# A ring for the transposed fields, longer product rings, and TensorE's sums in groups of two to four units

## The chip, the cores and the metric

The kernel runs on one core of a Trainium2 chip. The metric is the device time of one execution in microseconds. Five engines work beside each other, each through its own list of instructions in the order written: TensorE (PE), VectorE (DVE), ScalarE (ACT), GpSimd (POOL, here the issuer of gathers) and SyncE (SP, here the issuer of the other transfers). They meet only at semaphores.

## The reference

A recommendation model: 32 embedding tables of 64 columns are looked up for 1024 samples, all pairs of the 32 fields (496) go through a bilinear form of their own, and the 496 results with 16 dense inputs feed a network of three layers.

```python
e = stack([tbl_f[ids[:, f]] for f in range(32)], axis=1)      # 1024 x 32 x 64
p, q = e[:, ROW_IDX], e[:, COL_IDX]                            # the 496 pairs i < j
z = einsum('bne,hne,bnh->bn', p, kernel, q)                    # kernel: 64 x 496 x 64
h = concatenate([z, dense_ctx], axis=1)                        # 512 inputs
h = maximum(h @ W_top1 + b_top1, 0)                            # 512
h = maximum(h @ W_top2 + b_top2, 0)                            # 256
y = h @ W_top3                                                 # 1024 x 1
```

Everything is float32.

## The kernel before

The 1024 samples are taken in four chunks of 256. POOL gathers the rows of all fields (256 indirect transfers, four fields or one "quad" after the other), and TensorE transposes each quad (`transpose_quad`, line 520), so that a couple of fields lies across the 128 partitions with the samples along the row. VectorE copies the result from PSUM to `emb` (`keep_quad`, line 426).

The pairs of a chunk are cut into 64 units of equal arithmetic, in the order of the list `UNITS`. `bilinear` issues a unit's matmuls into one of three pairs of PSUM banks (`bil`, a ring of `BIL_RING` = 3 that the transposes share), and VectorE's `multiply` takes it out again, times the second field of each pair. There are three kinds:

- `inner` (8 in a chunk): the pairs within a quad, 8 recorded matmuls (line 552) and three VectorE products (lines 454 to 458);
- `fields` (32): pairs with the samples along the row, 8 recorded matmuls (line 552) and one product into `prod` (line 447);
- `batch` (24): pairs with the samples across the partitions, 4 recorded matmuls (line 537) and one product into `rows_prod` (line 438).

What is left is a sum over 64 elements. For a batch unit ScalarE does it by 16 activations with an accumulated output (`sum_rows`, line 365), or VectorE by a reduction (line 480) for the units that `SUM_UNITS` names. For the 40 inner and fields units of a chunk TensorE does it, by matmuls with a selector of ones: `reduce_batch`, line 572, four recorded matmuls a unit, that is two of the kernel's, each on 32 columns of the array. `slot_row` says which: the units alternate between column tiles 0, 1 and column tiles 2, 3. Before, these sums come in 20 batches of two units, each batch issued `REDUCE_LAG` = 3 units after its last unit.

When a chunk's sums are done, `turn` (line 587) transposes ScalarE's and VectorE's sums on TensorE. It waits for the last ScalarE sum of the chunk, and stands in TensorE's order a few units into the next chunk. The three layers of a chunk (`head`, lines 597 to 607) go between units of the next chunk, at `PIECE_UNITS`; those of the last chunk stand at the end (lines 633 to 665).

The order of TensorE's work around the change is written out by these tables: at each unit `u` the quads that are due are transposed, the unit is issued, then a batch of sums, then a piece of the head. Each use of `bil` waits until VectorE has emptied the pair of banks used three uses before. A chunk's unit `inner` of quad 1 waits for VectorE's copy of that quad's transposes.

Of the kernel before, what the change touches and what calls it, by code (L numbers as in the profile page):

```python
# [9 lines left out]
ALU = mybir.AluOpType  # L10
# [33 lines left out]

ORDER = ["", "ff", "bbbb", "bfbbfb", "fffbbfff", "bfbbfffbff", "bbffbbffbfbf", "fffbffbbfbffff"]


def unit_list():  # L50
# [21 lines left out]

SUM_UNITS = [8, 52]
VECTOR_SUMS = {max(v for v in range(NB) if BATCHED[v] <= u) for u in SUM_UNITS}
NV, NA = len(VECTOR_SUMS), NB - len(VECTOR_SUMS)

BIL_RING, PROD_RING, ROWS_RING, IN_RING = 3, 6, 4, 4
BATCH_UNITS = 2  # L80
BATCHES = NS // BATCH_UNITS
GROUP_BATCHES = 32 // BATCH_UNITS
REDUCE_LAG = 3
SUM_LAG = 2
SEL_WIDTH = 30 + 32
K_DMA = 8


def summed_before(u):
# [104 lines left out]

def reduce_unit(b):

    return unit_at((b + 1) * BATCH_UNITS - 1) + REDUCE_LAG


REDUCED_AT = {reduce_unit(b): b for b in range(BATCHES * CHUNKS) if reduce_unit(b) < NUNIT}  # L200
# [1 line left out]


PIECES = ["l1a", "l1b", "l2", "l3"]
PIECE_UNITS = [9, 14, 32, 56]
KEPT_BEFORE = [0, 2, 4, 6]
KEPT = 7

# [11 lines left out]
def interaction_tower(nc, ids, tables, dense_rows, k_blocks, w1, b1, w2, b2, w3, ident, selector, y):  # L220
    ctx = ExitStack()
    with ctx:
# [16 lines left out]
        w3_sb = sb("w3_sb", [P, MT2])  # L239
        k_sb = sb("k_sb", [P, 2 * NPART, P])  # L240
        gathered = sb("gathered", [P, 2, CT, FIELDS * EMBED])
        emb = sb("emb", [P, 2, COUPLES, CHUNK])
        prod = sb("prod", [P, PROD_RING, 2, BANK])
        rows_prod = sb("rows_prod", [P, ROWS_RING, 16, EMBED])
        inner = sb("inner", [P, IN_RING, 2, CHUNK])
# [39 lines left out]
        def inner_batch(n):  # L285

            q, k = divmod(n, QUADS)
            return summed_before(q * NU + FIRST_OF[k]) // BATCH_UNITS

        @block.sync  # L290
        def _(sp):
# [59 lines left out]
        def _(act):  # L351
# [40 lines left out]
            for u in range(NUNIT):  # L392
                if u >= SUM_LAG and UNITS[(u - SUM_LAG) % NU][0] == "batch":
                    sum_rows(u - SUM_LAG)
                if u in REDUCED_AT:
                    q, b = divmod(REDUCED_AT[u], BATCHES)
                    if b in (GROUP_BATCHES - 1, BATCHES - 1):
                        copy_z(q, b // GROUP_BATCHES)
# [19 lines left out]
        def _(dve):  # L418
            def keep_quad(n):
                q, k = divmod(n, QUADS)  # L420
                dve.wait_ge(quad_transposed, n + 1)

                banks = bil[BANKS_OF["quad", n]][:, :, 0:CHUNK].rearrange("p s (x b) -> p x s b", b=EMBED)
                out = emb[:, q % 2, 2 * k:2 * k + 2, :].rearrange("p c b -> p (c b)")
                out = out.rearrange("p (x s b) -> p x s b", s=2, b=EMBED)
                dve.tensor_copy(out, banks).then_inc(emb_kept, 1)  # L426

            def multiply(u):
                q, (kind, part, t) = u // NU, UNITS[u % NU]
                k, m, c = PARTS[part]  # L430
                x_y, e = bil[BANKS_OF["unit", u]], emb[:, q % 2, :, :]
                dve.wait_ge(unit_done, u + 1)
                if kind == "batch":
                    v = batched_before(u)
                    if v >= ROWS_RING:
                        free_rows(v - ROWS_RING)
                    row = gathered[:, q % 2, t, 2 * c * EMBED:(2 * c + 8) * EMBED].unsqueeze(1)
                    dve.tensor_tensor(rows_prod[:, v % ROWS_RING, :, :].rearrange("p (j x) h -> p j (x h)", j=2),  # L438
                                      x_y[:, :, :], row.to_broadcast([P, 2, BANK]), ALU.mult).then_inc(unit_multiplied, 1)
                    return  # L440
                a = summed_before(u)
# [9 lines left out]
                a, b = 2 * k, 2 * k + 1  # L451
                if n >= IN_RING:
                    dve.wait_ge(batch_reduced, inner_batch(n - IN_RING) + 1)
                dve.tensor_tensor(out[:, 0, :].rearrange("p (j b) -> p j b", j=2), x_y[:, :, 0:CHUNK],  # L454
                                  e[:, a:a + 1, :].to_broadcast([P, 2, CHUNK]), ALU.mult)
                dve.tensor_tensor(inner[EMBED:P, n % IN_RING, 0, :], x_y[EMBED:P, 0, CHUNK:BANK],  # L456
                                  e[EMBED:P, b, :], ALU.mult)
                dve.tensor_tensor(inner[0:EMBED, n % IN_RING, 0, :], x_y[0:EMBED, 1, CHUNK:BANK],  # L458
                                  e[0:EMBED, a, :], ALU.mult).then_inc(unit_multiplied, 1)

            def free_rows(v):

# [40 lines left out]
        def _(pe):  # L503
# [21 lines left out]
            def bilinear(u):  # L525
# [196 lines left out]
```

## Time and profile before

| | |
|---|---|
| median of 3 runs | 434.41 us (434.13 to 434.64) |
| the profiled execution | 433.44 us |
| its span, first to last instruction | 431.6 us, so 1.8 us lie around it |
| PE busy | 386.8 us, 90% |
| ACT busy | 350.7 us, 81% |
| DVE busy | 338.0 us, 78% |
| POOL busy | 242.2 us, 56% |
| granted TensorE clock | 0.999 of full speed |

The 40 slices of the page show POOL issuing gathers for the first 30, and PE at 9 tenths in nearly all slices from the seventh on. The trace has four points that cut the run into stretches: the four `turn`s start at 130.62, 227.34, 324.06 and 419.07 us. The first chunk (up to 130.62) starts slowly, since the gathers arrive one quad after the other, and has no head pieces in it. The second and third stretch take 96.72 us each. A busy PE is not a measure of work done: matmul ends are modelled, so the rows below are read by their starts. What a thing costs on PE is the time from its start to the next thing's start.

### The profile page before, as it was taken

The numbers are of one execution on the slowest core, as the hardware profiler recorded it, in microseconds if no ns is written. First come the engines' busy times: TensorE is split into PE (matmuls) and PEld (weight loads), VectorE is DVE, ScalarE is ACT, GpSimd is POOL, SyncE is SP. The second block draws the span as 40 slices with busy tenths as digits, with TensorE's granted clock in tenths as the row PEclk, the third lists the DMA queues.
The fourth block names the chain that finished last, engine by engine and source line by source line (L and its number), as shares of the span: only waits on it lengthen the run. The fifth ranks groups of instructions, "written<-read, shape, count | busy, mean of one in ns | idle before, by whom it ended". The sixth has DMA issues, their size and how long they took to land.

```text
span 431.6 us, 9783 instructions
## 1 busy us (share of the span) xinstructions
PE 386.8 (90%) x2912; PEld 218.4 (51%) x2912; DVE 338.0 (78%) x369; ACT 350.7 (81%) x2850; POOL 242.2 (56%) x260
## 2 busy tenths in 40 slices
PE   0224789999989999999989999999989999999997
PEld 0113344546454655645554655655555655655556
DVE  1033898999988879699888879699888869799841
ACT  1000799999994999999983999999974999999971
POOL 5777777777777777777777777777770000000000
PEclk9999999999999999999999999999999999999999
DMA  4677992111111111111111111111110000000000
GB/s 120 157 168 162 200 261 58 30 25 29 28 27 29 30 26 30 25 29 30 25 30 30 25 30 29 26 30 25 30 30 2 1 2 1 2 3 0 2 2 0
DMA packets 13637, 19.29 MB, mean 45 GB/s; under 512 B 5584, under 2 KB 6928, under 8 KB 13584
## 3 DMA queue, kind: packets, MB, share of 16 engines
q0 software_dynamic: 8192, 8.40, 10.0%
q1 hardware_dynamic: 5392, 10.27, 10.0%
q8 instruction: 23, 0.38, 0.3%
q14 instruction: 30, 0.25, 0.2%
HBM read 18.65 MB, written 0.00 MB: 43 GB/s over the span
## 4 chain that ended last, share of the span: by engine, by line
PE 66%; ACT 20%; POOL 5%; DVE 3%; issue 3%; DMA 2%; DVEq 0%
PE bil L552 24%; ACT rows_prod L365 19%; PE bil L537 16%; PE z_ps L572 13%; PE side_ps L597 5%; POOL gathered L345 5%; PE side_ps L602 3%; DVE prod L447 2%; PE bil L520 2%; DMA gathered<-in_tbl,ids_sb 1%; PE bil L633 1%; PE z_ps L587 1%; PE bil L657 1%; PE side_ps L607 1%; DVE rows_prod L438 1%
## 5 line engine op out<-in xcount | busy, mean ns | idle before, releaser
L365 ACT ACTIVATE rows_prod<-rows_prod 128x64 f32<-128x64 f32 x1408 | 336.1, 245 | 56.0 <-DVE rows_prod L438 56.0
L345 POOL DMA_INDIRECT gathered<-in_tbl,ids_sb x256 | 242.0, 945 | 80.3 <-issue 77.7
L365 ACT ACTIVATION_READ_ACCUMULATOR rows_prod<-rows_prod 128x1 f32 x1408 | 269.3, 191 | 0.0
L552 PE MATMUL bil<-emb,k_sb 64*128 64x256 f32 x1280 | 163.9, 392 | 6.3 <-DVE emb L426 5.5
L447 DVE TENSOR_TENSOR prod<-bil,emb 128x1024 f32<-128x1024 f32 x128 | 151.3, 1214 | 8.6 <-PE bil L552 8.4
L552 PEld LDWEIGHTS bil<-emb,k_sb 64*128 64x128 f32 x1280 | 120.0, 190 | 65.2 <-issue 38.8
L438 DVE TENSOR_TENSOR rows_prod<-bil,gathered 128x1024 f32<-128x1024 f32 x96 | 115.2, 1215 | 28.2 <-PE bil L537 27.8
L537 PE MATMUL bil<-k_sb,emb 64*128 64x512 f32 x384 | 99.6, 610 | 1.6 <-DVE inner L458 1.6
L572 PE MATMUL z_ps<-prod,sel_sb 128*32 128x512 f32 x576 | 86.0, 604 | 0.2 <-ACT z_sb L375 0.2
L537 PEld LDWEIGHTS bil<-k_sb,emb 64*128 64x128 f32 x384 | 33.5, 186 | 32.0 <-DVE prod L447 16.9
L520 PE MATMUL bil<-ident_sb,gathered 64*128 64x64 f32 x256 | 15.2, 241 | 33.1 <-DMA gathered<-in_tbl,ids_sb 33.1
L426 DVE COPY emb<-bil 128x512 f32<-128x512 f32 x32 | 21.8, 681 | 29.3 <-PE bil L520 29.2
L520 PEld LDWEIGHTS bil<-ident_sb,gathered 64*128 64x128 f32 x256 | 11.5, 145 | 55.7 <-issue 37.1
L572 PEld LDWEIGHTS z_ps<-prod,sel_sb 128*32 128x32 f32 x576 | 12.7, 108 | 42.4 <-issue 14.7
L454 DVE TENSOR_TENSOR prod<-bil,emb 128x512 f32<-128x512 f32 x32 | 21.9, 683 | 10.3 <-PE bil L552 10.3
L572 PE MATMUL z_ps<-inner,sel_sb 128*32 128x512 f32 x64 | 25.2, 604 | 0.0
L597 PE MATMUL side_ps<-z_sb,w_sb 128*128 128x256 f32 x96 | 22.3, 386 | 0.0
L597 PEld LDWEIGHTS side_ps<-z_sb,w_sb 128*128 128x128 f32 x96 | 17.7, 190 | 4.2 <-issue 2.0
L375 ACT ACTIVATE z_sb<-z_ps 128x512 f32<-128x512 f32 x8 | 4.8, 594 | 12.9 <-PE z_ps L587 11.0
L456 DVE TENSOR_TENSOR inner<-bil,emb 64x256 f32<-64x256 f32 x32 | 13.7, 427 | 0.4
L458 DVE TENSOR_TENSOR inner<-bil,emb 64x256 f32<-64x256 f32 x32 | 13.3, 417 | 0.4
L602 PE MATMUL side_ps<-h_sb,w_sb 128*128 128x256 f32 x48 | 11.2, 386 | 0.0
(31 smaller groups left out, 72.3 us busy)
## 6 DMA issues: line engine op xcount, KB each, us to landing
k_sb<-in_k_blocks SPq DMA_DIRECT2D x24, 256.0 KB, 4.8
gathered<-in_tbl,ids_sb POOLq DMA_INDIRECT x256, 2.4
k_sb<-in_k_blocks SPq DMA_DIRECT2D x8, 192.0 KB, 5.8
inner<-in_dense_rows SPq DMA_DIRECT2D x64, 1.0 KB
w_sb<-in_w SPq DMA_DIRECT2D x1, 1024.0 KB
k_sb<-in_k_blocks SPq DMA_DIRECT2D x8, 64.0 KB, 4.7
w_sb<-in_w SPq DMA_DIRECT2D x1, 512.0 KB
ids_sb<-in_ids SPq DMA_DIRECT2D x1, 128.0 KB, 2.0
```

Source lines behind the costliest of these rows:

```text
L345: pool.indirect_dma_start(gathered[:, q % 2, t, field * EMBED:(field + 1) * EMBED], None, tables[field], bass.IndirectOffsetOnAxis(ap=ids_ ...
L365: last = act.activation(row, row, ACT.Copy, accum_out=z_rows[:, t, half, col:col + 1])
L426: dve.tensor_copy(out, banks).then_inc(emb_kept, 1)
L438: dve.tensor_tensor(rows_prod[:, v % ROWS_RING, :, :].rearrange("p (j x) h -> p j (x h)", j=2), x_y[:, :, :], row.to_broadcast([P, 2, BANK ...
L447: dve.tensor_tensor(out, x_y[:, :, :], both.to_broadcast([P, 2, BANK]), ALU.mult)\
L454: dve.tensor_tensor(out[:, 0, :].rearrange("p (j b) -> p j b", j=2), x_y[:, :, 0:CHUNK], e[:, a:a + 1, :].to_broadcast([P, 2, CHUNK]), ALU ...
L520: last = pe.transpose(bil[BANKS_OF["quad", n]][:, s, at:at + EMBED], gathered[rows, q % 2, t, (2 * k + c) * P:(2 * k + c + 1) * P], ident_ ...
L537: last = pe.matmul(out[:, s, :], e[rows, m, t * P:(t + 1) * P], k_sb[rows, 2 * part:2 * part + 4, :].rearrange("p n h -> p (n h)"), start= ...
L552: last = pe.matmul(out[:, s, i * CHUNK:(i + 1) * CHUNK], k_sb[rows, n, :], e[rows, j, :], start=True, stop=True)
L572: last = pe.matmul(z_ps[32 * col:32 * (col + 1), :], sel_sb[:, 30 - r:62 - r], moving, start=r == 0, stop=bank == 0 and r == 30, tile_posi ...
L597: last = pe.matmul(bank[:, j * CHUNK:(j + 1) * CHUNK], w1_sb[:, g, n * P:(n + 1) * P], z_sb[:, g, :], start=g == 0, stop=g == GROUPS - 1)
L602: last = pe.matmul(bank[:, n * CHUNK:(n + 1) * CHUNK], w2_sb[:, g, n * P:(n + 1) * P], h1_sb[:, g, :], start=g == 0, stop=g == MT1 - 1)
```

## The change

- `emb` becomes a ring of 20 couples (`EMB_RING`, `emb_at`) in place of two chunks of 16. The room goes to the rings of products: `PROD_RING` 6 to 8, `ROWS_RING` 4 to 5.
- TensorE's sums come in 14 groups of 4, 3, 2, 2, 4, 2, 3, 2, 3, 3, 4, 3, 3 and 2 units (`SUM_GROUPS`) in place of 20 batches of two. Each is still issued three units after its last unit.
- The units of quads 3 to 7 stand in another order (`ORDER`); there are as many of each kind.
- VectorE sums three batch units of a chunk (`SUM_UNITS`) in place of two, so ScalarE sums 21 in place of 22.
- The head's second piece moves from unit 14 to 17, the others by one unit.

```diff
-ORDER = ["", "ff", "bbbb", "bfbbfb", "fffbbfff", "bfbbfffbff", "bbffbbffbfbf", "fffbffbbfbffff"]
+ORDER = ["", "ff", "bbbb", "fbbfbb", "bffffffb", "bffbbbfbfb", "bbfbffffbfff", "ffbbfbfbffffff"]
...
-SUM_UNITS = [8, 52]
+SUM_UNITS = [17, 30, 54]
...
-BIL_RING, PROD_RING, ROWS_RING, IN_RING = 3, 6, 4, 4
-BATCH_UNITS = 2
-BATCHES = NS // BATCH_UNITS
-GROUP_BATCHES = 32 // BATCH_UNITS
+BIL_RING, PROD_RING, ROWS_RING, IN_RING = 3, 8, 5, 4
+
+SUM_GROUPS = [4, 3, 2, 2, 4, 2, 3, 2, 3, 3, 4, 3, 3, 2]
+BATCHES = len(SUM_GROUPS)
+GROUP_ENDS = [sum(SUM_GROUPS[:b + 1]) for b in range(BATCHES)]
+GROUP_BATCHES = GROUP_ENDS.index(32) + 1
...
+EMB_RING = COUPLES + 4
+
+def emb_at(q, c):
+    return (q * COUPLES + c) % EMB_RING
...
+def group_end(b):
+    q, r = divmod(b, BATCHES)
+    return q * NS + GROUP_ENDS[r]
...
-    return unit_at((b + 1) * BATCH_UNITS - 1) + REDUCE_LAG
+    return unit_at(group_end(b) - 1) + REDUCE_LAG
...
-PIECE_UNITS = [9, 14, 32, 56]
+PIECE_UNITS = [9, 17, 33, 57]
...
-        emb = sb("emb", [P, 2, COUPLES, CHUNK])
+        emb = sb("emb", [P, EMB_RING, CHUNK])
...
                 if a >= PROD_RING:
-                    dve.wait_ge(batch_reduced, (a - PROD_RING) // BATCH_UNITS + 1)
+                    dve.wait_ge(batch_reduced, group_of(a - PROD_RING) + 1)
...
             def reduce_batch(b):
-                pe.wait_ge(unit_multiplied, unit_at((b + 1) * BATCH_UNITS - 1) + 1)
+                pe.wait_ge(unit_multiplied, unit_at(group_end(b) - 1) + 1)
                 q, r = divmod(b, BATCHES)
-                if b and r % GROUP_BATCHES == 0:
+                if b and r in (0, GROUP_BATCHES):
                     pe.wait_ge(z_copied, 2 * q + r // GROUP_BATCHES)
-                for a in range(b * BATCH_UNITS, (b + 1) * BATCH_UNITS):
+                for a in range(group_end(b) - SUM_GROUPS[r], group_end(b)):
```

In the listings of order the matmuls are those the kernel writes, each recorded twice in the trace; in the changed kernel line 542 is the transposes, 559 a batch unit, 574 a fields or inner unit, 594 the sums. First, TensorE's order from unit 53 of the first chunk to its end; before:

```order
L537 MATMUL bil<-k_sb,emb 128x512 x2
L552 MATMUL bil<-emb,k_sb 128x256 x4
L572 MATMUL z_ps<-prod,sel_sb 32x512 x4
L552 MATMUL bil<-emb,k_sb 128x256 x4
L537 MATMUL bil<-k_sb,emb 128x512 x4
L572 MATMUL z_ps<-prod,sel_sb 32x512 x4
L552 MATMUL bil<-emb,k_sb 128x256 x4
L537 MATMUL bil<-k_sb,emb 128x512 x2
L552 MATMUL bil<-emb,k_sb 128x256 x8
L572 MATMUL z_ps<-prod,sel_sb 32x512 x4
```

And now, from unit 51 to the same place:

```order
L574 MATMUL bil<-emb,k_sb 128x256 x4
L559 MATMUL bil<-k_sb,emb 128x512 x4
L574 MATMUL bil<-emb,k_sb 128x256 x4
L594 MATMUL z_ps<-prod,sel_sb 32x512 x3
L594 MATMUL z_ps<-inner,sel_sb 32x512
L594 MATMUL z_ps<-prod,sel_sb 32x512 x4
L559 MATMUL bil<-k_sb,emb 128x512 x2
L574 MATMUL bil<-emb,k_sb 128x256 x4
L559 MATMUL bil<-k_sb,emb 128x512 x2
L574 MATMUL bil<-emb,k_sb 128x256 x16
L594 MATMUL z_ps<-prod,sel_sb 32x512 x6
```

The sums of two units at a time (four matmuls) have become one of four units (eight matmuls) and one of three (six matmuls), and between these two now stand seven units without a break. In the later chunks a piece of the head stands in these seven.

Second, TensorE's order across the boundary of two chunks, right behind the rows above: transposes of quad 0 of the next chunk, the last two units and the next chunk's unit 0, sums, transposes of quad 1, unit 1, transposes of quad 2, unit 2, sums, and the turn. Before:

```order
L520 MATMUL bil<-ident_sb,gathered 128x64 x8
L552 MATMUL bil<-emb,k_sb 128x256 x12
L572 MATMUL z_ps<-prod,sel_sb 32x512 x4
L520 MATMUL bil<-ident_sb,gathered 128x64 x8
L552 MATMUL bil<-emb,k_sb 128x256 x4
L520 MATMUL bil<-ident_sb,gathered 128x64 x8
L552 MATMUL bil<-emb,k_sb 128x256 x4
L572 MATMUL z_ps<-prod,sel_sb 32x512 x4
L587 MATMUL z_ps<-ident_sb,z_rows 32x128 x16
```

And now:

```order
L542 MATMUL bil<-ident_sb,gathered 128x64 x8
L574 MATMUL bil<-emb,k_sb 128x256 x12
L594 MATMUL z_ps<-prod,sel_sb 32x512 x6
L542 MATMUL bil<-ident_sb,gathered 128x64 x8
L574 MATMUL bil<-emb,k_sb 128x256 x4
L542 MATMUL bil<-ident_sb,gathered 128x64 x8
L574 MATMUL bil<-emb,k_sb 128x256 x4
L594 MATMUL z_ps<-prod,sel_sb 32x512 x4
L609 MATMUL z_ps<-ident_sb,z_rows 32x128 x16
```

Nothing has changed its place here; the sums behind the next chunk's unit 0 are of three units (six matmuls) in place of two.

## Rows read from the trace of the kernel before

**Rows 1.** The stretches; columns are named in the first line.
```profile
core 0: us, PE busy (x) PEld busy (x) DVE busy (x) ACT busy (x) POOL busy (x), PEclk, DMA share, GB/s
85.00:130.62 45.62, 43.77 (x352) 23.20 (x350) 43.24 (x48) 45.57 (x379) 34.34 (x38) 1.00 0.14 28
227.34:324.06 96.72, 95.18 (x732) 53.93 (x728) 83.73 (x92) 87.54 (x713) 72.22 (x77) 1.00 0.15 28
```
**Rows 2.** The chain around the first turn: start, us, what.
```profile
115.29 15.29 ACT rows_prod L365 x128
130.62 1.08 PE z_ps L587 x32
```
**Rows 3.** PE's timeline, pitches of units, sums and transposes: start, us, what.
```profile
298.54 2.86 PE L552 MATMUL bil<-emb,k_sb 64*128 64x256 f32 x24
301.33 0.63 PE L572 MATMUL z_ps<-prod,sel_sb 128*32 128x512 f32 x3
...
328.00 1.99 PE L537 MATMUL bil<-k_sb,emb 64*128 64x512 f32 x8
329.92 1.06 PE L572 MATMUL z_ps<-prod,sel_sb 128*32 128x512 f32 x8
330.91 0.47 PE L520 MATMUL bil<-ident_sb,gathered 64*128 64x64 f32 x8
331.21 1.94 PE L537 MATMUL bil<-k_sb,emb 64*128 64x512 f32 x8
332.99 1.03 PE L552 MATMUL bil<-emb,k_sb 64*128 64x256 f32 x8
```
**Rows 4.** The chain near the end: two batches of sums together, then the turn.
```profile
417.22 1.85 PE z_ps L572 x16
419.07 0.92 PE z_ps L587 x32
```
**Rows 5.** PE's timeline at a batch of sums cut in two by a wait.
```profile
66.42 1.04 PE L572 MATMUL z_ps<-prod,sel_sb 128*32 128x512 f32 x2
67.48 0.62 PE L572 MATMUL z_ps<-inner,sel_sb 128*32 128x512 f32 x1
67.48 0.62 PE L572 MATMUL z_ps<-prod,sel_sb 128*32 128x512 f32 x2
...
68.47 1.12 PE L537 MATMUL bil<-k_sb,emb 64*128 64x512 f32 x3
```
**Rows 6.** PE's timeline at a chunk's first units.
```profile
318.98 0.46 PE L520 MATMUL bil<-ident_sb,gathered 64*128 64x64 f32 x8
320.98 1.13 PE L552 MATMUL bil<-emb,k_sb 64*128 64x256 f32 x8 [1.54 <-DVE emb L426]
```
**Rows 7.** DVE's timeline at the same place, and at the transposes at 330.91.
```profile
318.78 0.68 DVE L454 TENSOR_TENSOR prod<-bil,emb 128x512 f32<-128x512 f32 x1
...
320.25 0.67 DVE L426 COPY emb<-bil 128x512 f32<-128x512 f32 x1
...
331.45 0.68 DVE L426 COPY emb<-bil 128x512 f32<-128x512 f32 x1
```
**Rows 8.** DVE's timeline, pace of products and a reduction.
```profile
299.81 3.47 DVE L447 TENSOR_TENSOR prod<-bil,emb 128x1024 f32<-128x1024 f32 x3
303.21 1.20 DVE L480 TENSOR_REDUCE z_rows<-rows_prod 128x16 f32<-128x1024 f32 x1
```
**Rows 9.** PE's timeline at a run of five units.
```profile
79.19 1.13 PE L537 MATMUL bil<-k_sb,emb 64*128 64x512 f32 x4
80.16 2.76 PE L552 MATMUL bil<-emb,k_sb 64*128 64x256 f32 x24
82.78 1.13 PE L537 MATMUL bil<-k_sb,emb 64*128 64x512 f32 x4
```
**Rows 10.** DVE's timeline at the same place.
```profile
81.51 3.47 DVE L447 TENSOR_TENSOR prod<-bil,emb 128x1024 f32<-128x1024 f32 x3
```
**Rows 11.** PE's timeline at the transposes of quad 4, first chunk.
```profile
58.74 0.46 PE L520 MATMUL bil<-ident_sb,gathered 64*128 64x64 f32 x8 [0.84 <-DMA gathered<-in_tbl,ids_sb]
```

More of the change, by code:

```diff
@@ L71 @@
 FIRST_PARTS = [UNITS[u][1] for u in BATCHED if UNITS[u][2] == 0]
-SUM_UNITS = [8, 52]
+SUM_UNITS = [17, 30, 54]
 VECTOR_SUMS = {max(v for v in range(NB) if BATCHED[v] <= u) for u in SUM_UNITS}
 NV, NA = len(VECTOR_SUMS), NB - len(VECTOR_SUMS)
-BIL_RING, PROD_RING, ROWS_RING, IN_RING = 3, 6, 4, 4
-BATCH_UNITS = 2
-BATCHES = NS // BATCH_UNITS
-GROUP_BATCHES = 32 // BATCH_UNITS
+BIL_RING, PROD_RING, ROWS_RING, IN_RING = 3, 8, 5, 4
+SUM_GROUPS = [4, 3, 2, 2, 4, 2, 3, 2, 3, 3, 4, 3, 3, 2]
+BATCHES = len(SUM_GROUPS)
+GROUP_ENDS = [sum(SUM_GROUPS[:b + 1]) for b in range(BATCHES)]
+assert GROUP_ENDS[-1] == NS
+GROUP_BATCHES = GROUP_ENDS.index(32) + 1
 REDUCE_LAG = 3
@@ L103, in vector_sums_before, with group_of @@
     return q * NV + sum(1 for x in VECTOR_SUMS if x < r)
+def group_of(a):
+    q, r = divmod(a, NS)
+    return q * BATCHES + sum(1 for end in GROUP_ENDS if end <= r)
+def group_end(b):
+    q, r = divmod(b, BATCHES)
+    return q * NS + GROUP_ENDS[r]
 def unit_at(a):
@@ L287, in inner_batch @@
             q, k = divmod(n, QUADS)
-            return summed_before(q * NU + FIRST_OF[k]) // BATCH_UNITS
+            return group_of(summed_before(q * NU + FIRST_OF[k]))
         @block.sync
@@ L397, in _ @@
                     if b in (GROUP_BATCHES - 1, BATCHES - 1):
-                        copy_z(q, b // GROUP_BATCHES)
+                        copy_z(q, int(b == BATCHES - 1))
                 if u == min(HEAD_AT):
@@ L423, in keep_quad @@
                 banks = bil[BANKS_OF["quad", n]][:, :, 0:CHUNK].rearrange("p s (x b) -> p x s b", b=EMBED)
-                out = emb[:, q % 2, 2 * k:2 * k + 2, :].rearrange("p c b -> p (c b)")
+                at = emb_at(q, 2 * k)
+                out = emb[:, at:at + 2, :].rearrange("p c b -> p (c b)")
                 out = out.rearrange("p (x s b) -> p x s b", s=2, b=EMBED)
@@ L430, in multiply @@
                 k, m, c = PARTS[part]
-                x_y, e = bil[BANKS_OF["unit", u]], emb[:, q % 2, :, :]
+                x_y = bil[BANKS_OF["unit", u]]
                 dve.wait_ge(unit_done, u + 1)
@@ L443, in multiply @@
                 if a >= PROD_RING:
-                    dve.wait_ge(batch_reduced, (a - PROD_RING) // BATCH_UNITS + 1)
+                    dve.wait_ge(batch_reduced, group_of(a - PROD_RING) + 1)
                 if kind == "fields":
-                    both = e[:, c:c + 2, :].rearrange("p c b -> p (c b)").unsqueeze(1)
+                    both = emb[:, emb_at(q, c):emb_at(q, c) + 2, :].rearrange("p c b -> p (c b)").unsqueeze(1)
                     dve.tensor_tensor(out, x_y[:, :, :], both.to_broadcast([P, 2, BANK]), ALU.mult)\
@@ L450, in multiply @@
                 n = q * QUADS + k
-                a, b = 2 * k, 2 * k + 1
+                a, b = emb_at(q, 2 * k), emb_at(q, 2 * k + 1)
                 if n >= IN_RING:
@@ L454, in multiply @@
                 dve.tensor_tensor(out[:, 0, :].rearrange("p (j b) -> p j b", j=2), x_y[:, :, 0:CHUNK],
-                                  e[:, a:a + 1, :].to_broadcast([P, 2, CHUNK]), ALU.mult)
+                                  emb[:, a:a + 1, :].to_broadcast([P, 2, CHUNK]), ALU.mult)
                 dve.tensor_tensor(inner[EMBED:P, n % IN_RING, 0, :], x_y[EMBED:P, 0, CHUNK:BANK],
-                                  e[EMBED:P, b, :], ALU.mult)
+                                  emb[EMBED:P, b, :], ALU.mult)
                 dve.tensor_tensor(inner[0:EMBED, n % IN_RING, 0, :], x_y[0:EMBED, 1, CHUNK:BANK],
-                                  e[0:EMBED, a, :], ALU.mult).then_inc(unit_multiplied, 1)
+                                  emb[0:EMBED, a, :], ALU.mult).then_inc(unit_multiplied, 1)
             def free_rows(v):
@@ L532, in bilinear @@
                 wait_banks(("unit", u))
-                out, e = bil[BANKS_OF["unit", u]], emb[:, q % 2, :, :]
+                out = bil[BANKS_OF["unit", u]]
                 if kind == "batch":
@@ L536, in bilinear @@
                         rows = slice(s * EMBED, (s + 1) * EMBED)
-                        last = pe.matmul(out[:, s, :], e[rows, m, t * P:(t + 1) * P],
+                        last = pe.matmul(out[:, s, :], emb[rows, emb_at(q, m), t * P:(t + 1) * P],
                                          k_sb[rows, 2 * part:2 * part + 4, :].rearrange("p n h -> p (n h)"),
@@ L551, in bilinear @@
                             j = 2 * k + 1 if s == 0 else 2 * k
-                        last = pe.matmul(out[:, s, i * CHUNK:(i + 1) * CHUNK], k_sb[rows, n, :], e[rows, j, :],
+                        last = pe.matmul(out[:, s, i * CHUNK:(i + 1) * CHUNK], k_sb[rows, n, :], emb[rows, emb_at(q, j), :],
                                          start=True, stop=True)
```

## The prediction

> **What bounds the kernel now.** I read the table of stretches first. In a stretch between two turns (227.34 to 324.06) PE is busy 95.18 of 96.72 us, ACT 87.54, DVE 83.73: PE is the bound, and the most that lost waits can give back there is 1.5 us a chunk [rows 1]. In the first chunk there is no head, and three engines run level: from 85.00 to 130.62 PE is busy 43.77, DVE 43.24 and ACT 45.57 of 45.62 us [rows 1]. The chain goes over ACT there: 128 records (64 activations) in 15.29 us, so 16 activations, one batch unit, cost 3.82 us, and the first turn starts the moment ACT is done [rows 2]. But PE itself arrives, by the sum below, at about 130.2, so freeing ACT alone is worth 0.4 us at most: the two are tied.
>
> Then PE's timeline, by starts. Two units take 1.92 us and three 2.79 us before the sums begin [rows 3], so a unit costs 0.86 and each unbroken run of units 0.20 on top. A batch of sums (four matmuls of the kernel, two units) takes 0.99 us [rows 3]. Two batches back to back take 1.85 [rows 4], so a filled round of four column tiles costs 0.86 and the change of kind behind it 0.14. Transposes behind sums cost 0.30 to the next start, and the run behind them starts 0.05 cheaper (1.78 against 1.92) [rows 3]: 0.25.
>
> **What does a group of three cost?** The before never has six matmuls in a group, so this is the open price. A group of four is eight matmuls, two on each column tile: two full rounds, 1.85 [rows 4]. In a group of three two of the column tiles get two matmuls and two get one. From below: it costs by the matmul, 1.5 rounds, 1.28 + 0.14 = 1.42. From above: two whole rounds, 1.85. The nearest row is the batch that was cut in two: its first matmul ran alone from 66.42, and the other three, after the wait, took from 67.48 to 68.47, 0.99 us, as long as four do; the one alone took 1.04 [rows 5]. A round costs the same whether its tiles are filled or not. I take 1.85.
>
> The trace shows the 0.20 + 0.14 = 0.34 us lost around each batch of sums [rows 3, 4]. The Trainium skill, TensorEngine Tiling (Array Packing), Key Properties, says the same as a rule: changing the tiling mode, and not just the tile, drains the engine. By this rule alone fewer groups are a gain; it is a rival below.
>
> **The change, part by part.**
>
> *TensorE's sums, a chunk.* Removed: 6 changes to and fro. Batches go from 20 to 14 (6 x 0.14 = 0.84) and the runs of units between other work from 27 to 20 (7 x 0.20 = 1.40): -2.2 us. Added: rounds. Three groups of four and six of three take two rounds each, five of two take one: 18 + 5 = 23 against 20, +3 x 0.86 = +2.6. Transposes between two units, which cost 0.05 more than behind sums, get one fewer: -0.05. Sum: +0.3 us a chunk. The saving is eaten by half-empty rounds.
>
> *The boundary of two chunks.* Unit 1 of a chunk waits for DVE's copy of quad 1, which stands behind DVE's work for unit 0. From the start of quad 1's transposes (318.98) it takes 2.00 us to unit 1, where 0.24 to 0.30 would do: about 1.7 lost, of which the trace names 1.54 as a wait on that copy [rows 6]. DVE is late because it needs 1.13 a product, 3.40 for three [rows 8], and 1.47 for an inner unit (318.78 to 320.25) [rows 7], where PE needs 0.86. The group of three ahead of it now gives DVE one round more. Step by step from the start of the sums at unit 61, PE now comes to the transposes of quad 1 after 1.85 + 0.30 + 0.92 + 0.96 + 0.96 + 1.85 = 6.84 (before, with 0.99 twice, 5.1). DVE can copy some 0.5 behind them (330.91 to 331.45) and takes 0.68 [rows 3, 7]; so unit 1 starts after 8.05 (before 5.1 + 2.0 = 7.1). Two rounds cost 1.7 and the wait shrinks by 0.8, to 0.95. There are three such places, one of them in the first chunk.
>
> *The first chunk.* Up to 58.74 PE waits for gathers [rows 11], which the change doesn't touch. Next there is a second anchor: the sums for quad 4's inner unit wait for a small DMA and go on at 67.48 [rows 5]. That DMA stands in SP's queue behind the big loads, so I leave it at the same time. Before, PE has by then issued units 0 to 20, now only units 0 to 19. From 68.47 to the turn:
> - before: 46 units 39.6, 16 runs 3.2, 15 rounds of sums with their change 14.9, six transposes 1.55, together 59.3; waits 2.4 (1.7 of it at the boundary, the rest small ones); this gives 130.2, which agrees with a turn at 130.62 behind ACT;
> - now: 47 units 40.5, 13 runs 2.6, 18 rounds and 11 changes 16.8, six transposes 1.6: 61.5.
>
> To this come waits on a bank. A ring of three pairs holds PE back to DVE's pace once DVE is late: the fifth unit of the run at 79.19 started at 82.78, just behind the end of the product of three uses before, which began at 81.51 and takes 1.21 [rows 9, 10]. That cost 0.04 there; every further unit of a run costs DVE's pace less PE's, 1.13 - 0.86 = 0.27. Walked unit by unit with these prices, DVE's new reduction at unit 30 (1.20 [rows 8]) and the transposes of quad 6 among units 31 to 37 cost 1.5 (they wait 0.66 until DVE has emptied unit 31's banks, and unit 34 waits 0.85 more for unit 32's); the run of seven, units 55 to 61, costs 0.8; unit 42 0.1; the boundary 0.95. Together 3.4, so the first turn starts at 68.47 + 61.5 + 3.4 = 133.3, 2.7 later than 130.62 [rows 2].
>
> *ScalarE.* One batch unit fewer a chunk, 3.82 us [rows 2]; in the first chunk it would be ready at about 126.7. Nothing waits for it by then, so this gives 0. In later chunks ACT has 9 us to spare [rows 1].
>
> *VectorE.* One reduction more (1.2 us) beside 83.73 busy of 96.72 [rows 1]: hidden behind PE in later chunks, in the first it is in the walk above.
>
> *The rings.* DVE's waits for a free `prod` and `rows_prod` are near nothing before: in the stretches its idle time is PE's lead, not a full ring. With 8 slots and groups that end three units later than their last, a slot is again free before its turn comes: the product of unit 60 needs the group issued behind unit 54. The ring of 20 couples adds no wait: a couple is overwritten only by DVE itself, after the chunk's last reader. 0.
>
> *The head's pieces.* The second now stands behind unit 17; it needs ScalarE's first two h1 results. Counted from the turn, ScalarE starts its first sum after some 6 us and has three to do, 3 x 3.82, then the two results: 18.5. PE gets to unit 17's end, by the pitches above and 3.65 for the first piece, after 22.8. 0.
>
> **The sum.** First turn +2.7. Three further stretches +0.3 each, +0.8 (the last groups, now three rounds in place of two, are in it). The boundary's wait twice -0.8, -1.6. Together +1.9, say +2.0. The profiled execution took 433.44 us (its span 431.6 and 1.8 around it), so it becomes 435.4. It lies 1.0 below the median of the runs, which becomes 434.4 + 2.0 = 436.4.
>
> **The rivals.**
> - *A, only the changes of kind cost.* The sums cost by the matmul (1.42 for a group of three): each chunk then keeps the 2.2 us, the boundary keeps its whole wait. Later chunks: 3 x -2.2 = -6.6, the first +2.7 - 2.1 (2.5 rounds) + 1.0 (DVE holds PE back instead) = +1.6: about -5, 429.5. The Trainium skill's rule on the drain (TensorEngine Tiling (Array Packing), Key Properties) points here. It turns on one number: a group of three under 1.6 us. Against it: three matmuls took as long as four [rows 5]. This is the case on the other side.
> - *B, the extra rounds fall where PE would have waited.* If the boundary's 0.95 goes away too (3 x 0.95), because DVE is less late than the walk says, the sum is -0.9: 433.5 to 434. For it: the before's own waits are all DVE lateness [rows 6, 7]. Against it: the copy cannot start before the transposes.
> - *C, bank waits in the later chunks too.* Longer runs (five units at 38 to 42, four with an inner unit in them at 34 and 47) at 0.27 a unit in four places, three chunks: +3.2, 439.6. For it: 82.78 [rows 9]. Against it: in those chunks the head's pieces and the two-round groups let DVE catch up.
> - *D, ACT set the first chunk.* If the chain's word is taken and PE can follow, the first turn moves by up to 3.8 to 126.8, and the time is about 430. Against it: PE busy 43.77 of 45.62 there [rows 1]. I count it with A.
>
> **The numbers.** Forecast 0.58, with its own range 435.0 to 438.2; A and D 0.12; B 0.18; C 0.12. Within 0.2% (0.9 us) of the before is about what a measurement of this kernel can tell from no change. Slower by more: 0.55 of the forecast and C, 0.67. Faster: A and D, and a third of B, 0.18. Same 0.15. The range takes in B and most of C and leaves A out: 433.3 to 439.0.
>
> **What would show it.** Right: a group of six matmuls takes 1.8 to 1.9 us to the next start, as a group of eight does; the first turn starts at 132 to 134.5; stretches between turns are 96.0 to 96.7 us, with a wait of about 0.8 to 1.0 at unit 1; ACT waits before its copy of z ahead of the first turn; the last sums before the last turn take 2.7 in place of 1.85. Wrong: six matmuls under 1.6, or a first turn before 130.6, makes it faster; stretches over 97 make it slower than forecast.

## The result, and the profile after

| | before | changed |
|---|---|---|
| median | 434.37 us (433.81 to 434.77, 12 runs) | 436.07 us (435.36 to 438.0, 12 runs) |
| ratio to before | 1 | 1.0052 (95%: 1.0039 to 1.0065) |
| PE / DVE / ACT busy | 386.8 / 338.0 / 350.7 us | 392.4 / 343.6 / 335.2 us |

The change made the kernel 1.7 us slower by the medians; 436.4 was forecast. The twelve runs fall in two groups. In four the mean granted clock is 0.996 and the time 437.2 to 438.0; in the other eight it is 0.998 to 1.0, and the time 435.4 to 436.2. The profiled execution is one of the four (437.89 us, span 436.1). The profile before was of an execution 0.9 below its median (433.44 us, span 431.6), so the two profiles lie 4.5 us apart, more than the two kernels do.

The stretches of the changed kernel, columns as in [rows 1]:

```profile
85.00:135.46 50.46, 48.25 (x377) 26.03 (x377) 47.29 (x52) 43.05 (x358) 38.14 (x41) 1.00 0.13 28
135.46:231.78 96.32, 95.53 (x732) 55.61 (x728) 85.16 (x94) 83.62 (x681) 72.68 (x78) 1.00 0.13 28
231.78:328.11 96.33, 95.54 (x733) 55.60 (x729) 85.18 (x94) 83.62 (x681) 68.88 (x73) 1.00 0.13 27
```

The first turn moved from 130.62 [rows 2] to 135.46. The later stretches became 0.4 us shorter, 96.32 against 96.72 [rows 1], though PE is busy 0.36 us longer in each: the extra rounds took the place of a wait. The last sums before the last turn take 2.7 us (420.84 to 423.54) in place of 1.85 [rows 4], as forecast.

TensorE's timeline of the changed kernel in the first chunk: a group of four, then the run of seven units, then a group of three (start, us, what).

```profile
115.39 0.63 PE L594 MATMUL z_ps<-prod,sel_sb 128*32 128x512 f32 x3
...
117.24 1.13 PE L559 MATMUL bil<-k_sb,emb 64*128 64x512 f32 x4
118.20 1.03 PE L574 MATMUL bil<-emb,k_sb 64*128 64x256 f32 x8
119.07 1.02 PE L559 MATMUL bil<-k_sb,emb 64*128 64x512 f32 x4
119.93 4.52 PE L574 MATMUL bil<-emb,k_sb 64*128 64x256 f32 x32
124.37 1.91 PE L594 MATMUL z_ps<-prod,sel_sb 128*32 128x512 f32 x12
126.21 0.46 PE L542 MATMUL bil<-ident_sb,gathered 64*128 64x64 f32 x8
```

The group of four takes 117.24 - 115.39 = 1.85, the group of three 126.21 - 124.37 = 1.84: six matmuls cost what eight do. In the run of seven the first three units start 0.96 and 0.87 apart, the last four take 124.37 - 119.93 = 4.44, 1.11 each: from there PE goes at VectorE's pace, held by the three pairs of banks.

The boundary of two later chunks, which answers to [rows 6, 7]:

```profile
323.75 0.46 PE L542 MATMUL bil<-ident_sb,gathered 64*128 64x64 f32 x8
325.00 1.14 PE L574 MATMUL bil<-emb,k_sb 64*128 64x256 f32 x8 [0.79 <-DVE emb L448]
```
```profile
324.25 0.69 DVE L448 COPY emb<-bil 128x512 f32<-128x512 f32 x1
```

From the transposes to unit 1 it takes 1.25 us in place of 2.00, and the copy now starts 0.5 behind the transposes, as early as it can.

What the forecast had not counted is at the sums of quad 4's inner unit, which answers to [rows 5]:

```profile
64.29 1.06 PE L594 MATMUL z_ps<-prod,sel_sb 128*32 128x512 f32 x6
67.59 1.71 PE L594 MATMUL z_ps<-inner,sel_sb 128*32 128x512 f32 x2 [2.24 <-DMA inner<-in_dense_rows]
69.23 3.84 PE L574 MATMUL bil<-emb,k_sb 64*128 64x256 f32 x24
```
```profile
64.00:67.20 3.20, 1.35 (x10) 0.15 (x6) 3.17 (x5) 3.20 (x29) 2.29 (x4) 1.00 0.85 231
67.20:71.20 4.00, 3.61 (x12) 1.77 (x14) 0.67 (x1) 4.00 (x36) 3.09 (x4) 0.58 0.15 33
```

The DMA landed at 67.5, as before. But PE now waits 2.24 us for it, and behind this wait the granted clock is 0.58 over 4 us, most of them at 1.2 GHz (columns as in [rows 1], the clock third from the end). The one matmul that was left, its two records, takes 1.71 us, and the next three units 3.84 (before, three took 2.8). The matmul and the change behind it take 1.64 to the next start where 0.99 would do, and the three units 3.76 where 2.79 would: 1.6 us in all. The four executions with the lower clock are on average 1.9 us longer than the other eight; only this one of the four has a profile, so that the others lost it at the same place is inferred from their clock of 0.996.

### The profile page after: what moved, and what is told of

Its sections match the earlier page's. It is cut to its first block, busy times and chain, and to the rows that moved or that the text cites. A ratio compares the mean times of both kernels' runs of the same rounds, so it can differ in the third digit from the quotient of the medians.

```text
span 436.1 us, 9663 instructions
## 1 busy us (share of the span) xinstructions
PE 392.4 (90%) x2912; PEld 226.8 (52%) x2912; DVE 343.6 (79%) x377; ACT 335.2 (77%) x2722; POOL 241.9 (55%) x260
## 4 chain that ended last, share of the span: by engine, by line
PE 80%; POOL 7%; DMA 4%; DVE 4%; issue 3%; ACT 1%; SPq 0%; DVEq 0%
PE bil L574 31%; PE z_ps L594 19%; PE bil L559 17%; POOL gathered L366 7%; PE side_ps L619 5%; PE side_ps L624 3%; PE bil L542 2%; DMA inner<-in_dense_rows 2%; DVE rows_prod L460 2%; DMA gathered<-in_tbl,ids_sb 1%; PE bil L655 1%; ACT rows_prod L386 1%; PE z_ps L609 1%; DVE prod L469 1%; PE bil L679 1%
## 5 line engine op out<-in xcount | busy, mean ns | idle before, releaser
L386 ACT ACTIVATE rows_prod<-rows_prod 128x64 f32<-128x64 f32 x1344 | 320.9, 242 | 56.2 <-DVE rows_prod L460 56.2
L386 ACT ACTIVATION_READ_ACCUMULATOR rows_prod<-rows_prod 128x1 f32 x1344 | 253.3, 188 | 0.0
L574 PE MATMUL bil<-emb,k_sb 64*128 64x256 f32 x1280 | 166.6, 395 | 5.0 <-DVE emb L448 3.2
L574 PEld LDWEIGHTS bil<-emb,k_sb 64*128 64x128 f32 x1280 | 121.6, 192 | 59.6 <-issue 21.0
L559 PE MATMUL bil<-k_sb,emb 64*128 64x512 f32 x384 | 96.5, 600 | 0.3 <-DVE inner L480 0.3
L594 PE MATMUL z_ps<-prod,sel_sb 128*32 128x512 f32 x576 | 90.0, 600 | 0.0
L559 PEld LDWEIGHTS bil<-k_sb,emb 64*128 64x128 f32 x384 | 35.1, 188 | 25.4 <-issue 10.2
L542 PE MATMUL bil<-ident_sb,gathered 64*128 64x64 f32 x256 | 15.3, 242 | 32.6 <-DMA gathered<-in_tbl,ids_sb 31.8
L594 PEld LDWEIGHTS z_ps<-prod,sel_sb 128*32 128x32 f32 x576 | 17.5, 108 | 47.5 <-issue 30.5
L396 ACT ACTIVATE z_sb<-z_ps 128x512 f32<-128x512 f32 x8 | 4.7, 586 | 32.6 <-PE z_ps L609 32.6
L502 DVE TENSOR_REDUCE z_rows<-rows_prod 128x8 f32<-128x512 f32 (+1 forms) x20 | 15.1, 787 | 0.3
```

What stands on the lines that cost most here:

```text
L386: last = act.activation(row, row, ACT.Copy, accum_out=z_rows[:, t, half, col:col + 1])
L502: last = dve.tensor_reduce(z_rows[:, t, half, col:col + count], rows_prod[:, v % ROWS_RING, first:first + count, :], AXIS.X, ALU.add)
L542: last = pe.transpose(bil[BANKS_OF["quad", n]][:, s, at:at + EMBED], gathered[rows, q % 2, t, (2 * k + c) * P:(2 * k + c + 1) * P], ident_ ...
L559: last = pe.matmul(out[:, s, :], emb[rows, emb_at(q, m), t * P:(t + 1) * P], k_sb[rows, 2 * part:2 * part + 4, :].rearrange("p n h -> p (n ...
L594: last = pe.matmul(z_ps[32 * col:32 * (col + 1), :], sel_sb[:, 30 - r:62 - r], moving, start=r == 0, stop=bank == 0 and r == 30, tile_posi ...
```

## The experiments

Each was timed beside the kernel before on the same chip; ratios are to that.

**Pairs again (e1_pairs).** Does the grouping itself make it slower?

```diff
-SUM_GROUPS = [4, 3, 2, 2, 4, 2, 3, 2, 3, 3, 4, 3, 3, 2]
+SUM_GROUPS = [2] * 20
```

> The changed kernel with its sums in 20 groups of two again (rings, order of units and head's places stay). Theory (a group costs whole rounds of 0.86 us, 0.14 for the change behind it, and 0.20 for each run of units it cuts): a later chunk has 20 rounds in place of 23 (-2.6), 6 more changes (+0.8), 10 more runs and four more transposes standing between units (+2.2), together +0.5, and the wait at unit 1 returns to 1.7 (+0.8): stretches between turns of about 97.5 us against 96.3. The wait for the small DMA in the first chunk gets shorter, since the sums with unit 16 are issued two units later. Together about 438 us. Rival (sums cost by the matmul, only changes of kind matter): six more changes and cuts at 0.34 in each of four chunks, about 444 us. Rival (grouping is what made it slower, pairs give the old time back): 434.4 us.

Measured: 438.66 us, 1.0107 (1.009 to 1.0124); stretches 97.56 us. In this order of units the uneven groups are worth 1.2 us a chunk, because the pairs' ends cut more runs, by the theory's sum. The theory's size holds; both rivals fall. One of its terms came out smaller: unit 1 starts 1.6 us behind the transposes, so 1.3 us are lost there and not 1.7, and some 0.4 are lost elsewhere. So "undo the groups" is not the way back to 434.4: order and groups belong together.

**Fours (e2_fours).**

```diff
+SUM_GROUPS = [4] * 10
```

> The changed kernel with ten groups of four. Theory: 20 full rounds and only ten changes, so a later chunk's own sum is 92.7 us against 95.4; no sums stand between unit 0 and unit 1 of a chunk, so the wait there grows to some 2 us: stretches of about 94.8 against 96.3. In the first chunk the sums with unit 16 come at unit 23, past the landing of the small DMA, so that wait goes too and the first turn comes at about 131. Together about 429 us. Rival (VectorE's pace sets the later chunks once PE gets shorter: 85 us of work in a stretch, but in bursts): stretches of 96 and 434 us. A group takes 1.85 us to the next start, as a group of three does in the changed kernel.

Measured: 448.82 us, 1.0342 (1.0318 to 1.0367). My expectation failed by 20 us, and so did the rival by 15. The mean clock of the six runs is 0.987 to 0.996, so a few of the 20 us are the clock's: in the profiled execution (0.996) it falls to half behind a wait of 3.07 us for gathers, at 58.76 in the first chunk. The stretches have the full clock. A stretch takes 99.57 us, though PE is busy in it 95.09 and its own sum is 92.7:

```profile
238.00:337.57 99.57, 95.09 (x732) 55.22 (x728) 84.75 (x94) 83.94 (x681) 64.17 (x68) 1.00 0.13 24
```

TensorE's timeline shows where: the end of a run of eight units between sums, then five with transposes among them.

```profile
297.85 4.30 PE L574 MATMUL bil<-emb,k_sb 64*128 64x256 f32 x32
302.15 1.13 PE L559 MATMUL bil<-k_sb,emb 64*128 64x512 f32 x4
...
306.27 1.09 PE L574 MATMUL bil<-emb,k_sb 64*128 64x256 f32 x8
307.52 2.86 PE L574 MATMUL bil<-emb,k_sb 64*128 64x256 f32 x24 [0.16 <-DVE prod L469]
```

Four units in 4.30 us are 1.08 each, where PE alone needs 0.86. DVE's work in the stretch is only 84.75 us, so it is not the average that binds: VectorE catches up while TensorE does its other work, the sums above all, and where they stand far apart PE waits for banks in the run and VectorE idles behind it. I had priced these waits in the first chunk and left them out here, rival C's mechanism. A stretch lies 6.9 us above its own sum. I had counted 2.1 of this, the wait at unit 1, and it came (2.29). The other 4.8 are waits for banks, which I had put at nothing; C had priced them at 1.1 a chunk for the changed kernel.

**The groups without the new order (e4_groups_alone).**

```diff
-ORDER = ["", "ff", "bbbb", "fbbfbb", "bffffffb", "bffbbbfbfb", "bbfbffffbfff", "ffbbfbfbffffff"]
+ORDER = ["", "ff", "bbbb", "bfbbfb", "fffbbfff", "bfbbfffbff", "bbffbbffbfbf", "fffbffbbfbffff"]
-SUM_UNITS = [17, 30, 54]
+SUM_UNITS = [8, 52]
-PIECE_UNITS = [9, 17, 33, 57]
+PIECE_UNITS = [9, 14, 32, 56]
```

> The new groups and rings with the order of units, VectorE's sums and head's places of the kernel before. Theory: same 23 rounds and 14 groups, but the ends of the groups don't fall in with the transposes, so there are 23 runs and six transposes between units in place of 19 and one: a later chunk's own sum is 96.5 against 95.4, stretches of about 97.8, and the first chunk is 2.5 us longer: 443 us. Rival (the new order of units is of no account, the groups alone make the change): 436 us.

Measured: 450.36 us, 1.0391 (1.037 to 1.0412); stretches 101.09. The rival falls by 14 us. The theory has the direction and misses 7 us, 3.3 of them in each of the two stretches between turns. The reason there is the one above: from 235.08 to 336.17 PE waits six times for a bank, 2.1 us together as far as the profile names it, at the fifth unit of a run, at transposes behind a run, or at a unit behind transposes. The new order, with VectorE's sums and the head's places that go with it, is what makes the new groups bearable; the three were not taken apart.

**The rings alone (e11_rings_alone).** The changed kernel with order, sums, places and pairs of the kernel before. Against the kernel before, only the rings differ (products 8 and 5 in place of 6 and 4, `emb` a ring of 20 couples). The edit of the changed kernel:

```diff
-ORDER = ["", "ff", "bbbb", "fbbfbb", "bffffffb", "bffbbbfbfb", "bbfbffffbfff", "ffbbfbfbffffff"]
+ORDER = ["", "ff", "bbbb", "bfbbfb", "fffbbfff", "bfbbfffbff", "bbffbbffbfbf", "fffbffbbfbffff"]
-SUM_UNITS = [17, 30, 54]
+SUM_UNITS = [8, 52]
-SUM_GROUPS = [4, 3, 2, 2, 4, 2, 3, 2, 3, 3, 4, 3, 3, 2]
+SUM_GROUPS = [2] * 20
-PIECE_UNITS = [9, 17, 33, 57]
+PIECE_UNITS = [9, 14, 32, 56]
```

> The changed kernel's rings (20 couples, products 8 and 5) with the order of units, sums in pairs, VectorE's sums and head's places of the kernel before, so that the instructions stand as in the kernel before. Theory: no full ring held anything, so 434.4 us, as before. Rival (the wider rings let VectorE run ahead): 433 us or less.

Measured: 434.74 us, 1.0000 (0.999 to 1.001). The rings alone don't change the time. They may not be without effect on single executions: two of the eleven have a clock of 0.996 (435.19 and 435.56 us), against one of the 55 of the kernel before whose clock is known (433.87 us, none the longer for it). The profiled one is one of the two:

```profile
112.50 1.88 PE L559 MATMUL bil<-k_sb,emb 64*128 64x512 f32 x8
116.44 1.07 PE L594 MATMUL z_ps<-prod,sel_sb 128*32 128x512 f32 x8 [2.05 <-DVE rows_prod L460]
```
```profile
115.72 0.57 ACT L396 ACTIVATE z_sb<-z_ps 128x512 f32<-128x512 f32 x1
```
```profile
117.50:121.00 3.50, 3.50 (x15) 2.15 (x16) 1.23 (x1) 3.50 (x31) 2.58 (x4) 0.53 0.14 30
```

These sums write to `z_ps` again and wait (`z_copied`) until ScalarE has copied its first half; the product that they also need was done at about 112.9, by VectorE's timeline. The copy ends at 116.29, and the sums start 0.15 later, as they do in the kernel before (115.29 and 115.44, where the wait is 0.19). So ScalarE holds PE in the first chunk at a second place besides the turn. Behind the wait of 2.05 us the granted clock is 0.53 over 3.5 us.

**The small DMAs early (e3_dense).** In the changed kernel:

```diff
             for k in range(4, QUADS):
                 sp.wait_ge(emb_kept, k - 3)
                 load_k(k)
+            for n in range(IN_RING, 2 * IN_RING - 2):
+                place_dense(n)
             sp.dma_start(w1_sb[:, :, :], ...
...
-            for n in range(IN_RING, NQUAD):
+            for n in range(2 * IN_RING - 2, NQUAD):
                 place_dense(n)
```

> The changed kernel with the small DMAs of the dense inputs of quads 4 and 5 issued ahead of the head's weights. Theory: PE's wait of 2.2 us (and 3.3 from the first sums to the next unit) behind unit 19 goes, PE is up to 3.2 us earlier in the first chunk, the clock stays at 2.4 GHz there in every run, and nothing else changes: first turn at about 130.3, 432.6 us, and the spread between runs of 2 us goes. Rival (VectorE's pace sets the first chunk anyway): under 1 us gained, 435.0 us.

Measured: 434.34 us, 1.0007 (0.9993 to 1.002); by the two ratios 0.45% or 2.0 us less than the changed kernel. One run of twelve still had a clock of 0.996 (436.26 us) against four before, so the fall got rarer and did not go; where it came in that run no profile shows. The gain lies between theory (3.5 us) and rival (under 1): PE's wait is gone, but it runs into VectorE at once.

```profile
63.96 0.63 PE L596 MATMUL z_ps<-prod,sel_sb 128*32 128x512 f32 x3
...
64.96 1.13 PE L576 MATMUL bil<-emb,k_sb 64*128 64x256 f32 x8
66.47 2.27 PE L576 MATMUL bil<-emb,k_sb 64*128 64x256 f32 x16 [0.38 <-DVE prod L471]
```

The sums take 1.00 us here, but the unit behind the next one starts 1.51 after it in place of 0.96, waiting for a bank. The first turn comes at 131.37, 1.1 later than expected.

**What sets the first chunk (e7_before_dense, e8_before_sum3, e10_before_both).** The kernel before with the same edit, with a third reduction on VectorE, and with both:

```diff
-SUM_UNITS = [8, 52]
+SUM_UNITS = [8, 34, 52]
```

> The kernel before with the dense inputs of quads 4 and 5 placed ahead of the head's weights: PE's wait of 1.05 us at 66.42 goes. Theory (PE, VectorE and ScalarE are tied in the first chunk, the first turn waits for ScalarE): ScalarE works without a gap from 45.95 to 130.58 and isn't touched, so nothing is gained, 433.9 us. Rival (PE sets the first chunk): 1.0 us gained, 432.9 us.

> The kernel before with a third batch unit a chunk summed by VectorE (behind unit 34), ScalarE 21. Theory (tied): the first turn moves from 130.62 to about 130.3 at best, and VectorE's new reduction of 1.2 us puts PE back by up to as much in the first chunk: 433.7 to 434.9 us. Rival (ScalarE sets the first chunk, as the chain says): the first turn moves by up to 3.8 us, 430.1 us.

> The kernel before with both changes at once: dense inputs of quads 4 and 5 placed early, and VectorE summing a third batch unit. Apart they gave 0 and 0.6 us. Theory (ScalarE and PE are tied in the first chunk): together they give more than the sum, since each takes away the other's cover: the 1.05 us of e7's wait on top of e8's 0.6, less what VectorE's pace takes back, about 432.9 us. Rival (the first chunk is set by VectorE or the gathers): no more than e8 alone, 433.8 us.

| | median | ratio | first turn | ScalarE's last sum ends |
|---|---|---|---|---|
| e7 | 433.87 us | 0.9994 (0.9984 to 1.0004) | 130.69 | 130.64 |
| e8 | 433.84 us | 0.9986 (0.9977 to 0.9995) | 129.66 | 128.17 |
| e10 | 433.02 us | 0.9965 (0.9951 to 0.9979) | 129.54 | 128.04 |

The chain around the turn, of e7 and then of e8:

```profile
115.35 15.29 ACT rows_prod L367 x128
130.65 0.04 issue
130.69 1.08 PE z_ps L589 x32
```
```profile
128.85 0.99 PE z_ps L572 x8
129.84 0.87 PE z_ps L587 x32
```

With PE freed, ScalarE holds the turn at 130.69; with ScalarE freed, its last sum ends 2.4 us earlier, and PE comes 1 us earlier and holds the turn itself. Of this 1 us, 0.6 is there already at the sums of quad 4's inner unit: in e8's execution PE finds the small DMA landed at 66.89 and goes on at 67.89, in place of 68.47 [rows 5]. The two were tied, as forecast, and the 3.8 us that the chain seems to offer are not there (rival D). Both together give 0.35% (forecast 432.9, came 433.02), where the two apart give 0.06% and 0.14%. With intervals of 0.1% or more on each, it is not shown that the two together give more than their sum.

**Even groups in a fitting order (e5_even, e9_even57).** What the runs so far say is: full rounds only, and sums where VectorE is behind. This version has 13 groups, 20 rounds, the small DMAs early, and:

```diff
+ORDER = ["", "ff", "bbbb", "fbfffb", "bffbbbff", "bfbbbffbfb", "bbfffffbbfff", "fffbfffbbfbfff"]
+SUM_UNITS = [7, 26, 52]
+SUM_GROUPS = [4, 2, 4, 4, 2, 4, 2, 4, 2, 4, 2, 4, 2]
+PIECE_UNITS = [9, 22, 33, 60]
```

> The changed kernel with groups of 4 and 2 alone (13 of them, 20 rounds), an order of units in which no run between sums is longer than five, the ends of groups of four behind the runs in which VectorE falls back, the head's last pieces at other units, and the dense inputs of quads 4 and 5 placed early. Theory (full rounds, and sums where VectorE needs time): own sum of a later chunk 93.0 us against 95.4, about 1.4 of waits, so stretches of 94.4 against 96.3 and 96.7 in the kernel before; first turn at 129.3. Together about 426 us. Rival (PE's gain turns into waits for VectorE, as in the kernel with ten groups of four): stretches of 96.5 and about 433 us.

Measured: 431.69 us, 0.9931 (0.9919 to 0.9944), stretches 94.86 and the first turn at 129.92. The stretches are 0.5 and the first turn is 0.6 us above the forecast. Some 4 us are lost in the last chunk, at a place for which I had counted nothing:

```profile
403.89 2.86 PE L576 MATMUL bil<-emb,k_sb 64*128 64x256 f32 x24
409.27 2.04 PE L657 MATMUL side_ps<-z_sb,w_sb 128*128 128x256 f32 x4 [2.52 <-ACT y_sb L413]
411.11 3.34 PE L657 MATMUL bil<-z_sb,w_sb 128*128 128x256 f32 x12
```
```profile
408.60:412.10 3.50, 2.83 (x7) 2.33 (x8) 0.00 (x0) 3.50 (x31) 0.00 (x0) 0.54 0.00 0
```

A wait of 2.5 us for ScalarE, and again half the clock behind it (0.54). Four of the five runs have a clock of 0.996. So the last piece went back to unit 57:

> e5_even with the head's last piece back at unit 57 (it stood at 60). In e5_even's last chunk PE waited 2.5 us, from 406.7 to 409.3, until ScalarE, three sums behind, had copied that piece's result, and the granted clock fell to half for 3.4 us behind this wait. Theory: the wait goes and with it the slow stretch, some 2.5 + 1.8 us: 427.4 us, clock 0.99 or more of full speed in all runs but for the end. Rival (the clock falls there anyway, or the sums before it are late): 429.2 us or more.

Measured: 429.05 us (428.35 to 429.97, 4 runs), 0.9881 (0.9864 to 0.9898): 1.2% faster than the kernel before and the best of all. The profiled execution (428.35 us) has a clock of 1.0 and no wait at that place. One of the four runs still has 0.996. I expected 427.4, and the median is closer to the rival's 429.2; but the rival's reasons, a clock that falls there anyway or sums that are late, aren't in the profile. The last stretch became 3.8 us shorter (4.3 was forecast), and the two stretches before it grew by 0.6 each, to 95.45. The timelines show these 0.6, e5_even first and then e9_even57:

```profile
308.05 1.05 PE L631 MATMUL side_ps<-w_sb,h_sb 128*128 128x1 f32 x8
309.04 1.14 PE L576 MATMUL bil<-emb,k_sb 64*128 64x256 f32 x8
...
313.43 1.92 PE L596 MATMUL z_ps<-prod,sel_sb 128*32 128x512 f32 x16
```
```profile
305.31 1.05 PE L631 MATMUL side_ps<-w_sb,h_sb 128*128 128x1 f32 x8
...
311.01 3.13 PE L576 MATMUL bil<-emb,k_sb 64*128 64x256 f32 x24 [0.58 <-DVE rows_prod L462]
314.07 1.92 PE L596 MATMUL z_ps<-prod,sel_sb 128*32 128x512 f32 x16
```

At unit 60 the piece cut the run of units between two sums, and VectorE caught up during it. At unit 57 it stands right behind the sums, the run is whole, and PE waits for a bank.

**A half-empty round, by itself (e6_threes).** e5_even with every sum at the same place, and four times in a chunk 4 + 2 turned into 3 + 3:

```diff
-SUM_GROUPS = [4, 2, 4, 4, 2, 4, 2, 4, 2, 4, 2, 4, 2]
+SUM_GROUPS = [4, 2, 4, 3, 3, 3, 3, 3, 3, 4, 2, 3, 3]
+PLACES = [4, 6, 10, 14, 16, 20, 22, 26, 28, 32, 34, 38, 40]
-    return unit_at(group_end(b) - 1) + REDUCE_LAG
+    q, r = divmod(b, BATCHES)
+    return unit_at(q * NS + PLACES[r] - 1) + REDUCE_LAG
```

> The same kernel as e5_even, with every sum issued at the same place, but in four places of a chunk a group of 4 and one of 2 become two of 3. The matmuls, the changes of kind and the runs of units are the same; only four rounds of a chunk are half empty (24 in place of 20). Theory (whole rounds): 4 x 0.86 = 3.4 us a chunk more, in part given back as shorter waits for VectorE: stretches of 97.8, about 12 us slower than e5_even. Rival (sums cost by the matmul): no difference.

Measured: 442.22 us, 1.0179 (1.0166 to 1.0192), 10.5 us above e5_even by the medians; the two profiled executions, both with a clock of 0.996, are 11.8 apart, as the theory has it (about 12). Stretches 98.09 against 94.86, 3.2 for four rounds, 0.81 each. The timelines at the same places, e5_even and then e6_threes:

```profile
284.50 0.62 PE L596 MATMUL z_ps<-prod,sel_sb 128*32 128x512 f32 x1
...
285.50 1.13 PE L576 MATMUL bil<-emb,k_sb 64*128 64x256 f32 x8
...
289.14 1.92 PE L596 MATMUL z_ps<-prod,sel_sb 128*32 128x512 f32 x16
291.00 0.46 PE L544 MATMUL bil<-ident_sb,gathered 64*128 64x64 f32 x8
```
```profile
291.47 0.63 PE L598 MATMUL z_ps<-prod,sel_sb 128*32 128x512 f32 x3
...
293.31 1.13 PE L578 MATMUL bil<-emb,k_sb 64*128 64x256 f32 x8
...
296.96 1.91 PE L598 MATMUL z_ps<-prod,sel_sb 128*32 128x512 f32 x12
298.80 0.46 PE L546 MATMUL bil<-ident_sb,gathered 64*128 64x64 f32 x8
```

A group of two and one of four units cost 1.00 and 1.86; three and three cost 1.84 twice. The rival (cost by the matmul) said no difference; it is out.

## Why the prediction was right, step by step

- *The price of a group of three*, 1.85 from the cut batch [rows 5]: 1.84 in the profile after, and 0.8 us a round in e6_threes. This decided the sign. Rival A, under 1.6, is out.
- *TensorE's sums +0.3 a chunk, the boundary's wait -0.8*: together 96.2 was forecast for a stretch, 96.32 and 96.33 came. The wait at unit 1 went from 2.00 to 1.25 (forecast 1.2).
- *The first chunk*: forecast 133.3. Measured 135.46 in an execution in which the clock fell. Without the 1.6 us that the rows put down to the fall it would be 133.8; by the 1.9 us that lie between the two groups of executions, 133.6. There is no profile of an execution without the fall, so this is worked out and not read. The single waits came near their prices: at the transposes of quad 6 and behind them 0.84 and 0.58 (forecast 0.66 and 0.85), the run of seven 0.9 (forecast 0.8).
- *The missing term* is the clock. The walk let PE stand at the small DMA for more than 3 us (64.29 to 67.59), against 1.06 before (66.42 to 67.48), and counted that stop as lost time only. In the profiled execution it also cost half the clock for some us behind it, and four of twelve runs have that execution's clock. In the median it is worth some 0.2 us, so the forecast of 436.4 came out 0.3 too high even so: the eight other runs have a median of 435.9, 0.5 below it. That the median came so near is in part luck, since a term left out and a sum 0.5 too high went against each other. Where the 0.5 went is open. A candidate is a wait that the walk had only among its small ones: ScalarE's copy of the first half of z held PE 0.19 us in the profile before and 2.05 in e11_rings_alone, and in the changed kernel it ends at 120.41, 4 us before the sums that need it. How long that wait was in the other executions of the kernel before, nothing here shows.
- *ScalarE, the rings and the head's pieces at 0*: e11_rings_alone is at 1.0000, and freed ScalarE waits for the turn in the profile after. It ended its first chunk's sums at 128.06, later than the 126.7 of the forecast, which changed nothing. Its waits for the turn before the copies of z rose to 32.6 us from 11.0:

```profile
L396 ACT ACTIVATE z_sb<-z_ps 128x512 f32<-128x512 f32 x8 | 4.7, 586 | 32.6 <-PE z_ps L609 32.6
```

  D is out by e7 and e8. B did not happen: 1.25 us at the boundary is the copy behind its own transposes. C did not happen in the changed kernel (a stretch is 0.1 above the forecast), but its mechanism is the largest part of what made e2_fours and e4_groups_alone 15 and 16 us slower than the kernel before.

## What to carry to other kernels

Where small matmuls on column tiles run side by side, as the four tiles of 128x32 do here, count rounds, not matmuls: fill every round, and don't pay with half-empty ones for fewer changes of kind. Where PSUM is a short ring and the engine that empties it is slower per unit, the other work of TensorE is its time to catch up: spread it, and check each run of units by itself, since the averages (93 against 85 us here) hide waits of 7 us. And before moving work past a transfer that lands late, see how long TensorE then stands.

## What the runs showed of the hardware

A round of the sums, one matmul of 128x512 on each of four 128x32 column tiles, cost the same filled or half empty: groups of six matmuls took 1.84 us to the next start, of eight 1.85, of four 0.99 to 1.00.

TensorE's granted clock fell to half, 1.2 GHz, in the midst of steady work in five of the thirteen profiled executions, each time behind a wait: 2.24 us in the changed kernel, 3.07 in e2_fours, 2.52 in e5_even, 2.39 in e6_threes and 2.05 in e11_rings_alone. Over the 4.0 us behind it in the changed kernel and the 3.5 in e5_even the clock was 0.58 and 0.54 of full speed. The stop of 1.06 us in the kernel before [rows 5] did no such thing. The length of the wait alone doesn't decide: behind the waits of 2.29 us at unit 1 of each later chunk of e2_fours the clock stayed full. Eight runs of the changed kernel show 0.998 or more. Whether their wait was as long isn't known, since the small DMA landed at different times, at about 67.5 in the profiles of both kernels and at 66.84 in e11_rings_alone.
